# Third layer of a graph network: radial features of nodes loaded on ScalarE's queue beside the sums

## The reference

```
h = max(layernorm(x), 0)
radial, conical = h[:, :16], h[:, 16:32]
rows, cols = concat([src, dst]), concat([dst, src])
neighbor_sum = segment_sum(conical[cols], rows, N)
deg = clip(segment_sum(ones, rows, N), 1)
combined = concat([radial, neighbor_sum / deg], axis=1)
x = x + relu(combined @ W1 + b1) @ W2 + b2        # 32 -> 128 -> 32
```

## Time and profile before

| | us |
|---|---|
| median of 3 runs | 4690.81 (4682.08, 4690.81, 4690.91) |
| the profiled execution, its own time | 4694.78 |
| its span in the trace | 4693.0 |
| VectorE busy in the span | 2870.1 (61%) |
| GpSimd busy in the span | 3469.0 (74%) |
| TensorE busy in the span | 2328.5 (50%) |
| ScalarE busy in the span | 958.4 (20%) |

### The profile page before, as it was taken

One profiled execution on the slowest core, in us unless ns is written; L12 is line 12 of the kernel. 1 busy time (PEld: TensorE's weight loads), 2 busy tenths in 40 slices (PEclk: granted clock), 3 DMA queues, 4 the chain that ended last, 5 costly groups with the idle time before them and its releaser, 6 DMA issues. The chain is left out here.

```text
span 4693.0 us, 30595 instructions
## 1 busy us (share of the span) xinstructions
PE 2328.5 (50%) x8870; PEld 1409.5 (30%) x8870; DVE 2870.1 (61%) x3600; ACT 958.4 (20%) x1485; POOL 3469.0 (74%) x3151
## 2 busy tenths in 40 slices
PE   7820067775777730000622331177764677666562
PEld 3410034443555420000622331022221444443331
DVE  8866177775888756666311110166665899988783
ACT  0012022221445421111000000144442111111110
POOL 7777677774777747776588888777774777777777
PEclk9865555555989875555655555588886787877776
DMA  1035244441444432222122222344442111110100
GB/s 29 12 95 166 47 95 100 98 98 59 151 151 156 147 110 66 65 71 66 6 5 5 5 5 5 56 156 151 151 151 81 29 29 29 32 28 26 28 26 9
DMA packets 348969, 327.82 MB, mean 70 GB/s; under 512 B 223275, under 2 KB 295862, under 8 KB 347596
## 3 DMA queue, kind: packets, MB, share of 16 engines
q1 hardware_dynamic: 85600, 236.67, 14.0%
q0 software_dynamic: 144256, 45.62, 10.1%
q10 hardware_dynamic: 118944, 43.56, 3.9%
HBM read 170.38 MB, written 156.58 MB: 70 GB/s over the span
## 5 line engine op out<-in xcount | busy, mean ns | idle before, releaser
L1378 POOL DMA_INDIRECT sum_table<-e_add_rows,e_add_idx x392 | 612.7, 1563 | 142.4 <-issue 118.0
L536 POOL DMA_INDIRECT g_ring<-x_table,pos x392 | 412.3, 1052 | 173.7 <-issue 119.2
L536 POOL DMA_INDIRECT c_ring<-x_table,pos x392 | 398.9, 1018 | 175.8 <-issue 131.0
L1919 PE MATMUL g_pX<-w,g_h_T 128*128 128x512 f32 x784 | 438.2, 709 | 177.8 <-DVEq L1776 177.5
L536 POOL DMA_INDIRECT f_ring<-con_table,pos x392 | 419.3, 1070 | 134.5 <-issue 127.6
L1739 POOL DMA_INDIRECT out_x<-g_out_rows,end_index x392 | 426.7, 1088 | 119.5 <-issue 119.5
L536 POOL DMA_INDIRECT d_ring<-g_table,pos x392 | 389.4, 993 | 167.2 <-issue 124.0
L536 POOL DMA_INDIRECT b_ring<-h_table,src x392 | 405.9, 1035 | 132.9 <-issue 126.0
L345 POOL DMA_INDIRECT x_dst<-in_x,dst x392 | 400.3, 1021 | 134.2 <-issue 134.2
L1648 PE MATMUL f_pH<-f_T,w2in 128*128 128x448 f32 x672 | 319.8, 622 | 274.4 <-DVE f_T L1540 274.4
L1429 PE MATMUL e_pS<-e_values,e_equal 128*128 128x18 f32 x784 | 169.0, 378 | 379.8 <-DVEq L1403 379.8
(11 more groups left out here) (346 smaller groups left out, 5033.2 us busy)
## 6 DMA issues: line engine op xcount, KB each, us to landing
f_sums<-sum_table ACTq DMA_DIRECT2D x126, 238.0 KB
sum_table<-c_zero SPq DMA_DIRECT2D x39, 715.0 KB, 5.3
g_table<-c_g SPq DMA_DIRECT2D x42, 448.0 KB, 2.5
h_table<-a_xp SPq DMA_DIRECT2D x28, 560.0 KB, 3.7
a_x<-in_x SPq DMA_DIRECT2D x28, 448.0 KB, 5.9
b_h_node<-h_table ACTq DMA_DIRECT2D x28, 448.0 KB, 4.4
b_x_node<-in_x SPq DMA_DIRECT2D x28, 448.0 KB, 4.9
x_table<-b_x_node SPq DMA_DIRECT2D x28, 448.0 KB, 2.5
```

Of the source, the lines that this page charges most:

```text
L536: pool.indirect_dma_start(out=ring[:, t, :], out_offset=None, in_=table, in_offset=bass.IndirectOffsetOnAxis(ap=idx[:, c * C + t:c * C + t ...
L1378: pool.indirect_dma_start(out=g.sums[b], out_offset=bass.IndirectOffsetOnAxis(ap=aidx[:, c % 2, t:t + 1], axis=0), in_=add[:, c % 2, t, :] ...
L1919: last = nc.tensor.matmul(pX[d % 2][:, j * 512:(j + 1) * 512], tsb[:, 0, quad], g.w3[:, (2 * d + j) % 4, :], start=True, stop=True)
```

## The change

The load of radial features leaves `load_node` on SyncE and becomes a fourth load in ScalarE's `load(j)`, for node jobs alone, behind the three tables of sums. It is counted by the same semaphore `here[j % 2]`, whose expected value is now computed by `landed(j)`: 16 for each load of the jobs of that parity up to j, which is R loads for an edge job and R + 1 for a node job. The buffer `radn` is now chosen by the job's parity (`j % 2`), as the sums are, and not by the block's (`k % 2`). `n_here` counts the load of x alone, and VectorE waits for it in `second(j)`, before the output, and no longer in `first(j)`. No arithmetic changes.

```diff
--- before.py
+++ after.py
@@ -1478,6 +1478,11 @@
         more_set, filled, all_turned, rowed, back = (S(x) for x in ("more_set", "filled", "all_turned", "rowed", "back"))
         jobs = [job for c in range(EC) for job in (("n", 2 * c), ("n", 2 * c + 1), ("e", c))]
         J = len(jobs)
+
+        def landed(j):
+
+            return 16 * sum(R + (kind == "n") for kind, _ in jobs[j % 2:j + 1:2])
+
         block = ctx.enter_context(nc.Block())
 
         @block.sync
@@ -1485,7 +1490,6 @@
             g.sem.clear_before(sp)
             def load_node(k):
                 sp.dma_start(flat(x2[:, k % 2]), node_rows(g.X2, k)).then_inc(n_here[k % 2], 16)
-                sp.dma_start(flat(radn[:, k % 2]), node_rows(g.RN, k, CON)).then_inc(n_here[k % 2], 16)
 
             for k in range(2):
                 load_node(k)
@@ -1515,7 +1519,7 @@
         def _(dve):
             def first(j):
                 (kind, k), b = jobs[j], j % 2
-                dve.wait_ge(here[b], 16 * R * (j // 2 + 1))
+                dve.wait_ge(here[b], landed(j))
                 total = sums[:, b, 0]
                 for i in range(1, R):
                     nc.vector.tensor_tensor(total, total, sums[:, b, i], ALU.add)
@@ -1525,8 +1529,7 @@
                     nc.vector.tensor_tensor(total[:, :, CON:CW], total[:, :, CON:CW], g.deg[:, part(k)].unsqueeze(2), ALU.add)
                     radial = g.rad[:, part(k), :]
                 else:
-                    dve.wait_ge(n_here[k % 2], 32 * (k // 2 + 1))
-                    radial = radn[:, k % 2]
+                    radial = radn[:, b]
                 nc.vector.tensor_copy(comb[:, :, 0:CON], radial)
                 dve.drain()
                 nc.vector.tensor_scalar(deg[:].unsqueeze(2), total[:, :, CON:CW], 1.0, None, ALU.max)
@@ -1543,6 +1546,8 @@
                 kind, k = jobs[j]
                 x = x2[:, k % 2] if kind == "n" else g.xd[:, part(k), :]
                 dve.drain()
+                if kind == "n":
+                    dve.wait_ge(n_here[k % 2], 16 * (k // 2 + 1))
                 dve.wait_ge(out_sb, j + 1)
                 nc.vector.transpose(flat(tr), osb[:]).then_inc(out_used, 1)
                 dve.drain()
@@ -1600,6 +1605,8 @@
                 for i, table in enumerate(g.sums):
                     frm = edge_rows(table, k, CW) if kind == "e" else node_rows(table, k, CW, base=EPAD)
                     act.dma_start(sums[:, j % 2, i].rearrange("p t f -> p (t f)"), frm).then_inc(here[j % 2], 16)
+                if kind == "n":
+                    act.dma_start(flat(radn[:, j % 2]), node_rows(g.RN, k, CON)).then_inc(here[j % 2], 16)
 
             def hidden(j, ns):
                 for n in ns:
```

## The result

The changed kernel took **4667.18 us** (median of 5 runs, 4662.25 to 4671.94) where the kernel before took 4690.91 (5 runs, 4682.08 to 4693.36): ratio 0.9951, interval 0.9937 to 0.9966. The profiled execution took 4663.28 us, with a span of 4661.4.

What follows compares the result with a forecast made beforehand. VectorE's late last copy was taken to bound the third layer, GpSimd next. 13.1 less 1.7 contention less 0.4 gave 11.0 us: profiled 4694.78 becomes 4683.8, the median 4.0 lower, so 4680 us, range 4671 to 4691.

Steps and rivals of the forecast that it cites:

- what bounds, and where the wait goes: Third layer: GpSimd becomes later than VectorE and bounds; VectorE's copies of gathered rows then wait some us in many chunks.
- the number forecast: VectorE's last third-layer copy of gathered rows could start at 3551.4, not 3564.5: 13.1 us at most to win.
- GpSimd pays for VectorE's company: Third-layer gathers: 14 us of VectorE work now runs beside them, one scan (+1.4) and one addition (+0.3), ending GpSimd 1.7 us later.
- case C: Third-layer gathers: three additions a chunk each stretch a gather by 0.9 us, ending 23 us later, at 4714; chance 0.06.
- the term of 1.7: Third layer: GpSimd's last gather ends 1.7 us later through contention with VectorE, subtracted from the gain.
- the 0.4 for VectorE leading the last round: End of third layer: 0.4 us subtracted because VectorE, nearly tied with GpSimd, may still lead the last round.
- VectorE's side: VectorE's last third-layer copy 17.8 us earlier: 23.4 of TensorE's waits for f_T less 5.6 for the fourth issue.
- the 5.6 us for the fourth issue: ScalarE's queue: the added radial load delays its activation by 0.43 us in the even node job, in 13 chunks.
- A: Third layer: longer TensorE idle slows its matmuls, at most 1.5 us a chunk; 4682 to 4690 us; chance 0.27.
- B: ScalarE's queue: the radial load lands too late, after some 3263, so second() is late again; 4687 to 4691; chance 0.08.
- D: Third layer: GpSimd's 10 us of longer idle pieces go as well, so VectorE's 17.8 us bound: 4673; chance 0.07.

Runs made afterwards that it cites:

- the other two profiles: The changed kernel run twice more without an edit; ratios to the kernel before 0.9955 and 0.9960, third-layer stage 585.0 and 581.1 us.
- the second profile: The changed kernel run once more without an edit; ratio to the kernel before 0.9955, third-layer stage 585.0 us.

## Why the prediction was wrong

**Right: what bounds, and where the wait goes.** GpSimd became the bound, the copies at L1558 wait for it, and the last of them starts 1.4 us after the last gather (2.3 and 1.4 in the other two profiles). Of the 14.5 us by which VectorE came late, 13.1 were won, the number forecast. Rounds with half the gathers show the same from the other side.

**Wrong: the step "GpSimd pays for VectorE's company".** It took the gathers' 50.8 us above 0.94 each as a fixed toll of VectorE's work, about 4.0 a chunk (over 13 chunks it is 3.9, over all 14 3.6), added the 14 us of work that now run beside them, and had GpSimd end 1.7 us later. The toll is not fixed. A gather that starts inside an instruction of VectorE with two inputs in SBUF lasts until after its end; one that starts first is not held up. By the new wait in second(), behind the drain, VectorE's additions slid from 0.06 us ahead of a gather to within 0.01 us of its start, mostly behind it, in 12 of 13 rounds, at 0.46 us each. The gathers got 5.7 us less busy instead of 1.7 more, and these third additions of a chunk alone make 5.0 of it. Moving the wait ahead of the drain in the changed kernel brings the delay back, and one more wait behind the drain in the kernel before removes it. The case C had the mechanism right, that what falls beside a gather changes, and the sign wrong: it took time away. The records place the turn at some 0.02 us: in the second profile such gathers start up to 0.02 us after the addition and still took 0.95, while those of the even block, 0.03 us and more after, took 1.39 or 1.40.

The trace of the kernel before held this already. Of its 392 gathers 99 start inside an instruction of VectorE whose inputs both lie in SBUF, and these make 49 of the 50.8 us. The counterpart is the product at L1563, whose second input, f_pc, lies in PSUM: it takes 1.71 us, and all 12 gathers that start inside it took 0.94. One round, first VectorE and then GpSimd, with a gather inside the product and the next inside the scan:

```profile
3240.46 1.71 DVE L1563 TENSOR_TENSOR f_ends<-x_dst,f_pc 128x896 f32<-128x896 f32 x1
3242.24 2.02 DVE L1191 TENSOR_TENSOR_SCAN x_dst<-f_mask_after,f_ends 128x896 f32<-128x896 f32 x1
...
3241.47 0.94 POOL L536 DMA_INDIRECT f_ring<-con_table,pos  x1 [0.31 <-issue]
3242.72 2.32 POOL L536 DMA_INDIRECT f_ring<-con_table,pos  x1 [0.30 <-issue]
```

So the toll could have been laid out by instruction and not by chunk; on which side of an addition a gather falls, by hundredths of a microsecond, could still not be told beforehand.

So the sum is, in the first profile: 13.1 from lateness, 5.7 from the gathers' busy time, 1.6 from idle between gathers (127.6 to 126.0): 20.4 for the stage's 20.1. Against 11.0 forecast, the term of 1.7 cost 7.4 us, and the 0.4 for VectorE leading the last round was not needed. In the other two profiles lateness and busy time make 12.1 + 5.2 = 17.3 and 13.1 + 5.4 = 18.5; idle was 1.7 more and 1.9 less, the stage's end 1.0 shorter in the second, and 16.4 and 20.3 were won.

**Wrong in size, without effect: VectorE's side.** 17.8 us, against the 35.6 that half the gathers show. I counted TensorE's waits, which are gone as forecast (27 down to 15), and not that its matmuls got faster: the group at L1648 was busy for 319.8 us before and 304.3 after, and the stage's granted clock rose from 0.81 to 0.83. That this makes up the difference is argued from these sums; no run changed it alone, and how much of the 5.6 us for the fourth issue was paid stays open. The sentence that GpSimd is the bound all the same if VectorE's side is earlier still held.

**The other cases.** A, the wait moves to TensorE's clock: no. TensorE's idle at the chunks' beginnings did grow, in front of its transposes, from 30.5 to 52.4 us in all, and the matmuls were still faster than before. B, no earlier in effect: no, the radial load lands with the sums. D asked for GpSimd's longer idle pieces to go; they stayed, three in each profile, at 2 to 4.6 us before and 1.4 to 4.2 after. What makes these pieces is open: no run was made for it.

**The spread of runs** was about 10 us on either side, as much as the forecast gain; of the first 23.7 us some 3 to 5 are of that kind, since the three ratios mean 21 us and the three stages 19.

## What to carry to other kernels

When two engines are nearly tied, take the wait off the later one and then price the other one anew: its time beside the first is not a constant, but depends on which of two instructions starts first, by hundredths of a microsecond. Look at what stretches the instructions of the coming bound, and take that away where the other engine has a wait to pay for it: the reduce was worth 3 to 7 us of the stage, and nothing that the time shows, when all jobs had it, and 9 us or more of the stage when only those had it after which VectorE waits anyway. A wait belongs where it passes under running work, but the place that costs least on its own engine can cost more on another.

## What the runs showed of the hardware

- An indirect gather that GpSimd starts inside an instruction of VectorE with two inputs from SBUF lasts beyond its end: 1.40 us instead of 0.94 beside the two additions, 2.09 to 2.39 us beside a scan of 2.02. Started 0.01 us ahead of it, the gather takes 0.94, and so does one inside a product of 1.71 us with one input from SBUF and one from PSUM. Of the instructions with one input only copies stretched a gather in the trace of the kernel before (1.25 us inside the copy at L1553, up to 1.09 at L1530). The Trainium skill (SBUF — State Buffer, Who interferes with whom) has it that issue order decides who blocks, which this agrees with. There the Trainium skill infers of tensor_tensor that descriptor generation is spared; the gathers here as a whole are not, and which part of one is held up, the reading of its indices from SBUF or the making of its descriptors, no run shows.
- One more semaphore wait behind a drain, already satisfied, moved VectorE's next instruction by 0.07 us (1.28 us from transpose to transpose instead of 1.21); ahead of the drain it moved it by none.
- A reduce of 128x1428 to 128x476 elements, strided, took 1.75 to 1.79 us, the two additions it replaces 1.38. Gathers that start inside it took 0.94.
